# A graph attention kernel: gathers held back by landings instead of by spacers and TensorE's signals

## What is computed

```python
Q_h = (x @ Wq + bq);  K_h = (x @ Wk + bk);  V_h = (x @ Wv + bv)      # per node
E = (edge_attr @ We + be)                                            # per edge
score = K_h[src] * Q_h[dst] / sqrt(12) * E
score = exp(clip(score.sum(-1, keepdims=True), -5.0, 5.0))           # per edge and head
msg = V_h[src] * score
wV = segment_sum(msg, dst);  Z = segment_sum(score, dst)
return layernorm(x + wV / (Z + 1e-06))
```

## Time and profile before

| | us |
|---|---|
| median of 2 timed runs | 1071.3 |
| lowest and highest of them | 1071.09, 1071.5 |
| span of the profiled execution | 1231.7 |
| busy in it: TensorE, DVE, ACT, POOL | 824.3, 595.7, 457.8, 919.8 |
| TensorE's mean granted clock, share of 2.4 GHz | 0.808 |
| DMA packets, data moved | 124525, 153.29 MB |

### The profile page before, as it was taken

The page is one execution under the profiler, slowest core; times in us unless marked ns, Lnnn a source line. Parts: engine busy times, 40 slices in busy tenths (PEclk is TensorE's granted clock), DMA queues, the critical chain, the costliest instruction groups (busy, mean ns, idle before and its releaser), DMA issues.

```text
span 1231.7 us, 13818 instructions
## 1 busy us (share of the span) xinstructions
PE 824.3 (67%) x3375; PEld 455.9 (37%) x3375; DVE 595.7 (48%) x1583; ACT 457.8 (37%) x1094; POOL 919.8 (75%) x1572
## 2 busy tenths in 40 slices
PE   6518565986676666667676667666767676776763
PEld 4415232543343333333333334333333333333433
DVE  5104344954444464445444545445554545454645
ACT  3206232743343343333333334333434343433331
POOL 8882777167878778778787787887777877877783
PEclk9757787988877888887888787887878877878885
DMA  9922344454545445445444444444444444444321
GB/s 245 277 77 77 104 126 109 137 145 120 144 116 138 125 112 131 125 111 127 122 121 125 108 135 117 120 132 120 111 130 125 128 127 112 121 130 126 92 77 51
DMA packets 124525, 153.29 MB, mean 124 GB/s; under 512 B 57885, under 2 KB 92191, under 8 KB 124436
## 3 DMA queue, kind: packets, MB, share of 16 engines
q0 software_dynamic: 37008, 75.28, 23.9%
q1 hardware_dynamic: 80608, 73.74, 21.7%
q10 hardware_dynamic: 6822, 3.31, 1.0%
HBM read 142.26 MB, written 9.98 MB: 124 GB/s over the span
## 4 chain that ended last, share of the span: by engine, by line
POOL 37%; PE 22%; issue 16%; another core or an unknown queue 10%; DVE 6%; DMA 6%; ACT 2%; SPq 0%; DVEq 0%; POOLq 0%
POOL kv L493 30%; POOL spacer L500 7%; DMA kv<-kv_table,src_idx 5%; PE ps_eq L1030 4%; PE ps_eq L1023 4%; PE ps_qe_seg L1055 3%; PE ps_last L1055 3%; PE ps_eq_qe L1023 2%; PE ps_qe_seg L1041 2%; PE ps_eq_qe L1030 1%; PE ps_eq_qe L1041 1%; DVE ps_last L768 1%; DVE node_stage L743 1%; DMA w_all<-biases_in 1%
## 5 line engine op out<-in xcount | busy, mean ns | idle before, releaser
L493 POOL DMA_INDIRECT kv<-kv_table,src_idx x750 | 714.2, 952 | 285.5 <-issue 114.7
L602 ACT ACTIVATE ps_last<-clipped 128x32 f32<-128x32 f32 x196 | 39.4, 201 | 542.4 <-issue 397.2
L1030 PE MATMUL ps_eq<-pick_t,q_win 128*96 128x512 f32 (+1 forms) x262 | 169.5, 735 | 78.7 <-ACT e_t L597 58.4
L761 DVE TENSOR_TENSOR kq<-kv,ps_qe_seg 128x384 f32<-128x384 f32 x98 | 53.9, 550 | 260.7 <-DMA kv<-kv_table,src_idx 195.7
L1023 PE MATMUL ps_eq<-ea,w_all 128*96 128x512 f32 (+1 forms) x262 | 172.5, 747 | 8.1 <-issue 7.4
L500 POOL MEMSET spacer<- 128x128 f32 x782 | 172.8, 221 | 2.7 <-remote 2.2
L761 DVE TENSOR_TENSOR kq<-kv,ps_eq_qe 128x384 f32<-128x384 f32 x98 | 54.1, 552 | 238.3 <-DMA kv<-kv_table,src_idx 175.5
L1055 PE MATMUL ps_qe_seg<-node_stage 128*104 128x80 f32 x784 | 116.2, 306 | 54.5 <-issue 28.9
L1055 PE MATMUL ps_last<-node_stage 128*104 128x80 f32 x780 | 108.2, 292 | 49.3 <-issue 24.2
L588 ACT ACTIVATE distance<-rel_bc,neg_part 80x512 bf16<-80x512 bf16 x196 | 138.4, 706 | 1.8 <-issue 0.6
L1055 PEld LDWEIGHTS ps_qe_seg<-node_stage 128*104 128x104 f32 x784 | 105.2, 218 | 64.6 <-issue 49.6
(11 more groups left out here) (90 smaller groups left out, 788.2 us busy)
## 6 DMA issues: line engine op xcount, KB each, us to landing
ea<-ea_t_in SPq DMA_DIRECT2D x196, 192.0 KB
rel_bc<-rel_rows_dram SPq DMA_DIRECT2D x196, 80.0 KB
kv<-kv_table,src_idx POOLq DMA_INDIRECT x750
q_win<-q_table SPq DMA_DIRECT2D x196, 30.0 KB
kv_table<-node_stage SPq DMA_DIRECT2D x5, 576.0 KB
x_both<-x_t_in SPq DMA_DIRECT2D x5, 480.0 KB, 8.9
x_both<-x_rows_in ACTq DMA_DIRECT2D x10, 240.0 KB
out<-node_stage SPq DMA_DIRECT2D x11, 192.0 KB
```

Of the source, the lines that this page charges most:

```text
L493: pool.indirect_dma_start(rows[0:n, :], None, table, bass.IndirectOffsetOnAxis(ap=src_idx[0:n, tile:tile + 1], axis=0)).then_inc(semaphore ...
L761: nc.vector.tensor_tensor(kq[:, group % 2, 0:n, :], kv[:, slot, 0:n, 0:DIM], ps_qe[group % 2][:, 0:n * DIM].rearrange("p (t d) -> p t d", ...
L1030: nc.tensor.matmul(ps_eq[(2 * group + 1) % 3][0:DIM, 0:n], q_win[:, slot, :], pick_t[:, group % 3, 0:n], start=True, stop=True).then_inc(e ...
```

## The change

The spacers go, and with them the tile, its semaphore and the four waits on TensorE. Instead `room_for` makes each gather wait until the gather two before it has landed (`IN_FLIGHT = 2`), in the early stage too. As a wait for one gather needs a semaphore that no other gather in flight adds to, `e_kv` is now one semaphore for each tile of a group (four in all) instead of one for each slot of the ring (16). So `times_keys` and `early_transpose` wait for each tile's semaphore. The wait for the ring (`e_msg`) now stands in front of every group from 16 on.

```diff
-PACED_FROM = 32
+IN_FLIGHT = 2
@@ semaphores and tiles
-        spacer = sb("spacer", [P, 128], F32)
-        e_kv = [sem(f"e_kv{i}") for i in range(KV_RING)]
+        e_kv = [sem(f"e_kv{t}") for t in range(GROUP_TILES)]
-        e_space = sem("e_space")
@@ gpsimd
-            def space(tile):
-                if tile:
-                    pool.wait_ge(e_space, tile)
-                nc.gpsimd.memset(spacer[:], 0.0).then_inc(e_space, 1)
+            def landed(group, t):
+                pool.wait_ge(e_kv[t], 16 * (group + 1))
+            def room_for(group, t):
+                if group * GROUP_TILES + t >= IN_FLIGHT:
+                    landed(*divmod(group * GROUP_TILES + t - IN_FLIGHT, GROUP_TILES))
 
             pool.wait_ge(l_src_early, 16)
             for group in range(EARLY):
                 for t in range(GROUP_TILES):
-                    gather(kv[:, group, t, 0:DIM], x_rows, group, t, e_kv[group])
-                    space(group * GROUP_TILES + t)
+                    room_for(group, t)
+                    gather(kv[:, group, t, 0:DIM], x_rows, group, t, e_kv[t])
...
                 for group in range(EARLY, GROUPS):
-                    slot, ahead = group % KV_RING, min(group + 2, GROUPS - 1)
-                    if KV_RING <= group < PACED_FROM:
+                    slot = group % KV_RING
+                    if group >= KV_RING:
                         pool.wait_ge(e_msg, group - KV_RING + 1)
                     for t in range(tiles_of(group)):
-                        if group >= PACED_FROM:
-                            pool.wait_ge(*((e_seg, group - 3), (e_e, ahead + 1), (e_q, ahead + 1), (e_turn, group + 1))[t])
-                        gather(kv[:, slot, t, :], kv_table, group, t, e_kv[slot])
-                        space(group * GROUP_TILES + t)
+                        room_for(group, t)
+                        gather(kv[:, slot, t, :], kv_table, group, t, e_kv[t])
@@ vector, times_keys
-                fetched = sum(tiles_of(g) for g in range(slot, group + 1, KV_RING))
-                dve.wait_ge(e_kv[slot], 16 * fetched)
+                for t in range(n):
+                    dve.wait_ge(e_kv[t], 16 * (group + 1))
@@ tensor, early_transpose
-                pe.wait_ge(e_kv[group], 16 * GROUP_TILES)
+                for t in range(GROUP_TILES):
+                    pe.wait_ge(e_kv[t], 16 * (group + 1))
```

More of the change, by code:

```diff
@@ L150, in build @@
     assert SUMS * FINAL_TILES + WINDOW <= 512 and LAG_TRANSPOSE == SUMMED + 2
-    assert KV_RING > 2 * SUMMED and PACED_FROM >= KV_RING
+    assert KV_RING > 2 * SUMMED
     assert EARLY < KV_RING and tiles_of(EARLY) == GROUP_TILES
```

## The result

| | before | after |
|---|---|---|
| median, us | 1071.3 | 1384.5 |
| span of the profiled execution | 1231.7 | 1382.0 |
| ratio, 95% interval | | 1.292 [1.289, 1.296] |

The changed kernel is 29% slower. The sign was forecast, the size was not: 1140 was predicted, and 1384.5 lies far above the range of 1050 to 1210.

What follows compares the result with a forecast made beforehand. Bound taken as POOL's gather cadence, 1.335 us. Forecast: table gathers start at 62.7, plus 749 steps of 1.41, plus 16.4 to the end, plus 4.3, about 1140 us, 6.4% slower; range 1050 to 1210, 8 in 10.

Steps and rivals of the forecast that it cites:

- What bounds the kernel before: POOL's cadence of 1.335 us a gather, summing to 1067.0 us plus 4.3; 170.8 us of waits put down to the profiled execution.
- The sign that I called the sharpest: Profiled span of the changed kernel falls from 1231.7 to about 1150 us, near the median, though the median rises.
- Spacers out: 782 spacers go from POOL; if nothing else held a gather, the step would be 0.95 to 1.12 us.
- Pacing out: Dropping POOL's waits on TensorE gains nothing in timed runs; in a profile up to 170.8 us less the ring's cost.
- The landing chain: Gathers on POOL wait for the last but one's landing: step (L + d)/2 = 1.41 us against 1.335.
- L: Time from a gather's start to its landing, taken as 2.54 us; pieces in the trace had mean 2.88.
- d: Time from a landing to the start of the gather that waited for it, taken as 0.28 us.
- the signs of being wrong: Wrong if the mean step is under 1.335 us, or old timed runs held TensorE waits; then the landing chain gains.
- step 2: Pacing term: from group 16 on gathers still wait for the ring's `e_msg`, a wait over long before.
- my rival of coupled landings: One late landing holds both gathers behind it: step 1.48 to 1.58 us, 1229 us in total; chance 0.14.
- The early stage: 32 early gathers beside the table loads: between 5 us gain and 27 loss, +12 taken, table gathers from 62.7 us.
- Semaphores: Three more checks of about 0.05 us a group on DVE: nothing, as it has 2 us to spare; 29 uncovered.

Runs made afterwards that it cites:

- b_light: Kernel before, TensorE's feature and query matmuls made for 128 of 512 edges from group 8 on: 1071.9 us, kernel before there 1071.7.
- b_looser: Kernel before, each of the four waits on TensorE's progress asked for one group earlier, spacers kept: 1071.7 us, kernel before there 1071.7.
- b_nopacing2: Kernel before without the waits on TensorE's signals, spacers kept, on a fast chip: 1073.4 us, kernel before there 1073.4.
- b_smallea: Kernel before with edge features loaded for one partition only from group 8 on: 1071.9 us, kernel before there 1071.7.
- b_nopacing: Kernel before without the waits on TensorE's signals, spacers kept, on a slow chip: 1284.0 us, kernel before there 1213.7.
- a_same: Changed kernel without further edit, run where the kernel before takes 1230.5 us: 1376.8 us, ratio 1.119.
- a_ringquad: Changed kernel with the ring's wait only in front of every fourth group: 1332.0 us, kernel before there 1213.7.
- a_twowaits: Changed kernel with a second, already fulfilled ring wait at each group's third gather from group 16 on: 1446.0 us, kernel before there 1230.5.
- a_smallea: Changed kernel with edge features loaded for one partition only from group 8 on: 1342.7 us, kernel before there 1230.5.
- a_early4: Changed kernel with four gathers in flight in the early stage, two afterwards: 1360.6 us, kernel before there 1230.5.
- a_three: Changed kernel with three gathers in flight instead of two: 1280.4 us, kernel before there 1213.7.

## Why the prediction was wrong

**What bounds the kernel before: half right.** That its timed executions went at 1.335 us a gather, at 1067 + 4.3, held: b_light, b_looser, b_nopacing2 and b_smallea all stay at 1072 to 1073, and b_nopacing2 shows the cadence. But the waits of 170.8 us did not belong to the profiler. For every edit the profiled span agrees with the timed median, and the profile of the kernel before has the waits that mark TensorE's stops, which the traces of b_nopacing2, b_looser, b_light and b_smallea don't have at all:

```profile
ACT e_t L597 <- remote: 79.4, 26, 13.6
...
DVE acc_t L797 <- remote: 21.7, 7, 5.8
```

So the profile I read was in all likelihood of an execution like those on the chips where the kernel before takes 1214 and 1230, near its span of 1231.7, and the timed runs of 1071 were not. Nothing names the chip of that profile, so this is inferred and not shown. The sign that I called the sharpest, a span of about 1150, failed: it was 1382.0, near its median, as the forecast said, but above 1231.7. The signs of POOL alone held: busy 743.1 (745 forecast), idle until landings, no wait on DVE L782 in its list.

**Spacers out: mis-sized.** 0.95 to 1.12 was the step without them; it is 1.25. This term was hidden behind the landings and did not enter the sum.

**Pacing out: right** where the kernel before takes 1071 to 1073 us (b_nopacing2, 1.000), wrong where TensorE stops (b_nopacing, 5.8%), which I had among the signs of being wrong and not among the rivals. Even there the landing chain did not gain, as that sign said it would: a_same is 12% slower.

**The landing chain: right in its mechanism, wrong in two of its sizes.** This is the step that failed: (L + d)/2 with L = 2.54 and d = 0.28.
- d was right for one restart of a group (0.26) and 0.46 too small for the other (0.74): in the 180 groups from 16 on about 83 us. I had counted the waits as if one gather had one, while the ring's wait of step 2 stands at the same gather as the landing's. I had costed it at nothing since it is fulfilled; a_ringquad and a_twowaits show that it is the second wait itself that costs.
- L was 2.94 and not 2.54: 187 x 2 x 0.39, about 148 us. The pieces in the earlier trace rows had a mean of 2.88, and I discounted it as the choice of the chain. There was nothing to discount: the landings that the trace has, on the chain or not, have a mean of 2.90. Two of them and the two restarts make 6.80 of the 6.87 us of a group. So the step came near that of my rival of coupled landings (1.48 to 1.58, at 0.14), but not for its reason: that a late landing holds more than its own successor is worth at most the 0.07 that are left. a_smallea puts 34 us of the landings on the feature loads; why the rest are later than 2.54 is open.
- Together these are the 231 us of 749 x 0.308. As 2.94 is what the step leaves beside the restarts, that sum proves nothing by itself; the directly read 2.90 does.

**The early stage: right in kind, small in size.** +27 us was the upper bound, +12 was taken, and the table gathers began at 77.5: +26.8, 14.8 us more than in the sum. a_early4 shows it on the chain.

**Semaphores:** DVE and TensorE are hardly on the new chain (1% and 0%), so what their waits cost does not show, as said.

**The range** had its upper end at a step of 1.50. Both the mean of the pieces and the doubled wait lay outside it; with 2.88 for L and 0.28 and 0.74 for the restarts the step would have been 1.695, and the sum 62.7 + 749 x 1.695 + 16.4 + 4.3 = 1353.

## What to carry to other kernels

A wait for the landing of the n-th last transfer turns the latency into the cadence: it is landing plus restart over n, and the landing to put in is the measured mean with the collisions in it, not one near the least. Give it enough in flight that even a late landing fits (here four), and don't let two waits meet on one gather. Before a profile's waits are put down to the profiler, ask whether the profile and the timed runs could come from different chips: the median of runs and the span of the profile 15% apart was the sign. And a change that wins on one chip needs a run on the other kind.

## What the runs showed of the hardware

- In none of the 20 traces do two gathers start closer than 1.24 us; the usual least is 1.25 (0.95 for the instruction and 0.30 between). With a memset between them it is 1.335.
- A gather of 128 rows landed 2.90 us after its start in the mean (374 gathers of the changed kernel, least 2.51, most 4.53).
- A gather that waits for a landing alone starts 0.26 us after it; with a second semaphore to wait for it is 0.74, even if that one is long fulfilled (groups before and from 16 on in one trace, a_twowaits).
- On chips where the kernel before takes over 1200 us, TensorE's results came late by several us at a time, up to 13.4 in DVE's waits, when it had room to run ahead (b_nopacing, a_three), and not on others. On the former, kernels that differ by 29% elsewhere differ by 12%. What makes it stop was not found.
